# Third of five graph layers: edge projection and edge transposes ahead of the node products in TensorE's order

## The reference, cut to what matters

```
def _sage_conv(x, src, dst, Wl, b, Wr):
    agg  = segment_sum(x[src], dst)            # sum of the neighbours' rows
    cnt  = segment_sum(ones, dst)
    mean = agg / maximum(cnt, 1)[:, None]
    return mean @ Wl + b + x @ Wr

x = layernorm(x + conv2(relu(conv1(x))))                 # layers a1, a2: 128 -> 128 -> 128
x = layernorm(x + conv3(relu(conv2(relu(conv1(x))))))    # layers b1, b2, b3: 128 -> 256 -> 256 -> 128
```

## Time and profile before

| what | us |
|---|---|
| median of 3 runs | 5009.95 (5004.19 to 5011.4) |
| the profiled execution's own time | 5021.73 |
| its span (first to last instruction) | 5020.1 |
| TensorE busy in the span | 4645.7 (93%) |
| VectorE busy | 3822.4 (76%) |
| ScalarE busy | 2614.3 (52%) |
| stage of the third layer, 1634 to 2540 us after the start | 906 |
| stage of the fourth layer, 2541 to 3977 | 1436 |

### The profile page before, as it was taken

How to read it: one execution, slowest core, us unless ns; L and a number is a source line. 1 busy time by engine, 2 the same in 40 slices (tenths; PEclk the granted TensorE clock), 3 DMA queues, 4 the chain that set the end, 5 groups by cost and what they waited for, 6 DMA issues and landing times. The chain is left out here.

```text
span 5020.1 us, 145464 instructions
## 1 busy us (share of the span) xinstructions
PE 4645.7 (93%) x38674; PEld 4547.9 (91%) x38675; DVE 3822.4 (76%) x10162; ACT 2614.3 (52%) x7279; POOL 2329.1 (46%) x2182
## 2 busy tenths in 40 slices
PE   1788787999999899999989999999999899999998
PEld 1777776999999799999979999999999899999998
DVE  4566664777778699999967777777777588888888
ACT  1344443888988344444423333333333277777777
POOL 2666664555553444444344444444444343334331
PEclk9999898999999899999989999999999899999999
DMA  1667665888888566666668888888888788889887
GB/s 42 162 182 189 177 183 151 234 234 235 233 234 229 160 205 205 208 206 205 203 187 256 256 254 255 256 253 255 255 254 255 211 243 258 257 259 261 261 260 219
DMA packets 1454117, 1109.89 MB, mean 221 GB/s; under 512 B 76260, under 2 KB 1384833, under 8 KB 1454022
## 3 DMA queue, kind: packets, MB, share of 16 engines
q1 hardware_dynamic: 1377418, 927.61, 61.5%
q0 software_dynamic: 75712, 180.66, 14.5%
q10 hardware_dynamic: 892, 0.40, 0.0%
HBM read 696.86 MB, written 411.51 MB: 221 GB/s over the span
## 5 line engine op out<-in xcount | busy, mean ns | idle before, releaser
L1402 ACT ACTIVATE f_t_hi_b<-f_turned_b 128x512 fp32r<-128x512 f32 x588 | 332.3, 597 | 933.3 <-PE f_turned_b L1300 739.5
L1329 PE MATMUL f_product_b<-b_r_all,f_t_hi_b 128*128 128x256 f32 x2352 | 709.4, 302 | 1.1 <-DVE f_onehot_b L1450 1.1
L1442 DVE SCALAR_TENSOR_TENSOR f_t_lo_b<-f_turned_b,f_t_hi_b 128x512 fp32r<-128x512 f32 x588 | 388.1, 687 | 395.6 <-ACT f_t_hi_b L1402 326.5
L975 DVE TENSOR_TENSOR m_onehot_a<-iota_all,t_win_all 128x512 f32<-128x512 f32 (+1 forms) x588 | 455.9, 776 | 275.1 <-PE m_product_a L842 194.8
L753 POOL DMA_INDIRECT m_e_rows_b<-g,m_e_idx_b x392 | 395.7, 1009 | 574.9 <-ACT m_e_idx_b L881 506.0
L1331 PE MATMUL f_product_b<-b_r_all,f_t_hi_b 128*128 128x256 f32 x2352 | 660.5, 281 | 0.0
L1333 PE MATMUL f_product_b<-b_r_all,f_t_lo_b 128*128 128x256 f32 x2352 | 660.3, 281 | 0.0
L1255 POOL DMA_INDIRECT f_e_rows_b<-x,f_e_idx_b x392 | 392.8, 1002 | 508.0 <-ACT f_e_idx_b L1387 435.4
L1336 PE MATMUL f_product_b<-f_ring_b,f_onehot_b 128*128 x3136 | 621.8, 279 | 0.0
L1407 ACT ACTIVATE f_ring_b<-f_e_product_b,t_rec_all 128x256 f32 (+1 forms) x784 | 329.7, 472 | 526.2 <-PE f_e_product_b L1357 405.6
L753 POOL DMA_INDIRECT m_e_rows_a<-h,m_e_idx_a x392 | 398.2, 1016 | 390.0 <-ACT m_e_idx_a L881 311.4
(11 more groups left out here) (210 smaller groups left out, 12336.9 us busy)
## 6 DMA issues: line engine op xcount, KB each, us to landing
g<-f_rows_out_b SPq DMA_DIRECT2D x392, 512.0 KB
f_rows_in_b<-g SPq DMA_DIRECT2D x196, 512.0 KB
m_rows_in_b<-g SPq DMA_DIRECT2D x196, 512.0 KB
m_t_full_a<-in_x_flat_dram SPq DMA_DIRECT2D x196, 256.0 KB
h<-m_rows_out_a SPq DMA_DIRECT2D x196, 256.0 KB
m_rows_in_a<-h SPq DMA_DIRECT2D x196, 256.0 KB
m_res_in_a<-in_x_dram SPq DMA_DIRECT2D x196, 256.0 KB
x<-m_rows_out_a SPq DMA_DIRECT2D x196, 256.0 KB
```

What stands on the lines that cost most here:

```text
L975: v.tensor_tensor(onehot[:, s, n0:n0 + n, :], pr.iota[:, :].unsqueeze(1).to_broadcast([P, n, P]), pr.t_win2[:, bass.ds(g.n(0, WINDOWS) + n ...
L1329: pe.matmul(to, t_hi[:, s, k, cols], cv["r2"][:, k, 0, :], start=(t % per == 0 and k == 0), stop=False, skip_group_check=True)
L1402: act.activation(t_hi[:, s, k, :], turned[(s * kt + k) % 2][:, :], FUNC).then_inc(s_hi.sem, 1)
L1442: v.scalar_tensor_tensor(out=t_lo[:, s, k, :], in0=turned[(s * kt + k) % 2][:, :], scalar=0.0, in1=t_hi[:, s, k, :].bitcast(F32), op0=ZERO_OP,
```

## The change

The third layer gets the flag that the fourth already has. On TensorE alone, `places(g)` and `multiply(g, 0)` move behind `project` and `turn_edges`; the step becomes `turn_nodes(g+1)`, `project(p-1)`, `turn_edges(p+1)`, `places(g)`, `multiply(g, 0)`, `multiply(g, 1)`. No instruction is added or removed, and no other engine's order changes.

```
-            dict(name="b1", h=x1, out=g1, relu=False, w=1, f_out=256, turned=False, Wl=b_wl1, Wr=b_wr1, b=b_b1),
+            dict(name="b1", h=x1, out=g1, relu=False, edges_first=True, w=1, f_out=256, turned=False, Wl=b_wl1, Wr=b_wr1, b=b_b1),
```

## The result

The changed kernel takes 5129.4 us (median of 4 runs, 5121.3 to 5135.68) against 5007.07 (4999.8 to 5011.4) of the kernel before in the same comparison: ratio 1.0249 [1.0237, 1.0262], 122 us slower. The forecast was 20 us slower.

What follows compares the result with a forecast made beforehand. The prediction took the pace at which TensorE takes matmuls as the bound. A two-group loop of 5.00, 0.05 and 4.07 us gave 4.56 against 4.456 a group, +19.6 us over 188 groups: 5010 + 20 = 5030 us, range 5006 to 5050.

Steps and rivals of the forecast that it cites:

- `places` moves behind the edge transposes: TensorE's 592 ns register load: twelve matmuls, some 1.4 us, cover it; costed at nothing, uncovered at most 18 us in all.
- the projection moves from T + 1.62 to T + 0.35: T starts a group's node transposes; the projection waits for VectorE's ring low part, making 4.56 us a group, +19.6 us.
- the 20 to 30 named as the sign: Third layer's steady groups: TensorE waits for the ring's low part some 0.1 us a group, 20 to 30 us in all.
- the first rival: No stall: VectorE moves forward with its inputs and only the turn-end gaps go; 5004 us, chance 0.12.
- second rival: Faster outright: TensorE's matmul spacing falls to 0.113 us, gaining 28 us; 4982 us without the stall, chance 0.05.
- The one-hot matrices and the gather: TensorE's waits: one-hot matrices' gets 0.9 us looser, the gather's 1.2 us tighter, costed at nothing as gathers run ahead.
- The turn ends' gaps: Idle ahead of the node transposes at turn ends goes when the register load moves: 5.8 us, not added to the sum.
- The stalled projection at full clock: A weight load nothing hides after the projection's wait: 0 to 0.17 us a stall, up to 16 us; 0 taken.
- The third rival: Heavier stall: TensorE's signal reaches ScalarE 0.93 us late on every second group's node transposes; +44 us, 5074 us, chance 0.09.
- The fourth rival: The stall comes, but pieces closing up elsewhere in TensorE's group make up half; +7 to +14, 5017 to 5024 us, chance 0.08.

Runs made afterwards that it cites:

- nodes_proj: Kernel before with the projection, then the ring places' load, moved behind the node transposes, edge transposes staying between the product halves; 4888.56 against 4772.92 us, ratio 1.0242.
- quarter_store: Changed kernel storing one of four node tiles per group in the third layer, the rest filled behind its loop; 4.730 us a group, 5394.35 us with the fill.
- plain_new: Changed kernel with the third layer's GpSimd gathers replaced by SyncE's plain loads of fixed rows; 4869.68 against 4774.24 us, 4.935 us a group.
- low_early: Changed kernel with VectorE's low part of the ring moved two instructions earlier in the third layer; 4910.41 against 4774.24 us, ratio 1.0283, 5.139 us a group.
- load_behind_nodes: Kernel before with only the ring places' load moved behind the node transposes in the third layer; 5008.89 against 5008.36 us, ratio 0.9996, 4.428 us a group.
- early_load2: Changed kernel with VectorE's ring low part earlier and the ring places' load between node transposes and projection; 4776.67 against 4772.92 us, ratio 1.0006.

## Why the forecast was wrong

**The step that failed is "*`places` moves behind the edge transposes* ... twelve matmuls stand between ... and they cover it", costed at nothing.** The twelve matmuls are between in the program, but most of them are through, or held with it, when the load is made. The sequencer passes instructions on in order, and at a weight load whose semaphore hasn't come it stops; the register load behind it starts only with the release, 0.16 us behind the awaited instruction's end in five kernels in which the edge transposes are ahead of it, and in nodes_proj 0.11 us behind the projection's start. In the changed kernel that is 0.44 us behind the projection's start (mean of 90 groups), when the projection and the edge transposes have 0.5 us left; a load of 0.59 us and the 0.15 us to the product don't fit under that. The cover of the register load is the queued work behind the last wait that ends late, not all the work ahead of it. The forecast priced the loss of cover at 0.59 us once a turn; it is lost in every second group, and at 1.17 us. Two things were missed with it:
- The wait that now stands ahead of the load, edge transposes for the low part of the gathered rows, wasn't looked at, since TensorE's own waits show it nowhere. VectorE writes that low part next behind the ring's: 2007.79 + 0.41 = 2008.20, 0.17 us ahead of the load.
- The load was taken at 592 ns from the earlier trace rows. Its place moved into the store. The trace of before had the other duration, one layer on, in the order that the third layer was to get:

```profile
L1306 PEldq TENSOR_LOAD <-t_slot_all x189: 587/765/1945, 2601.3 to 3956.0; - x189
```

It costs nothing there because the ring's low part is 1.6 us early and nothing ahead of the load waits: the load starts 1.06 us behind the end of the gathered rows' low part (median of 188), not 0.16.

**The sum, term by term,** in us a group. The first two terms are differences between kernels; the last two are estimates from durations in the changed kernel and in quarter_store:

| term | from | us a group | x 188 |
|---|---|---|---|
| the ring's wait | 4.589 - 4.457 | 0.132 | 25 |
| a load of 0.59 us in the open | 4.730 - 4.589 | 0.141 | 27 |
| the store stretches it | (1.172 - 0.593) / 2 | 0.290 | 54 |
| ScalarE late behind the node transposes | (0.910 - 0.655) / 2 | 0.128 | 24 |
| sum | | 0.691 | 130 |
| measured | 5.122 - 4.457 | 0.665 | 125 |

The halves are for the loop over two groups, which closes once. The 1.172 is the mean load in the groups that wait and the 0.910 ScalarE's mean start behind T in those that don't, both in the changed kernel; 0.593 and 0.655 are the same two in quarter_store. As a test, plain_new has no late ScalarE and loads of 1.046 us in the groups that wait: 4.730 + 0.453 / 2 = 4.957; it measures 4.935. The terms aren't wholly independent: without the ring's wait (low_early) the loads are longer still, 1.40 us, and the distance is the same.

**Right:** *the projection moves from T + 1.62 to T + 0.35* and waits for the ring's low part; it starts 0.05 us behind the low part (2007.87 to 2007.93), and the loop alone is 4.589 us against 4.56. That the view's 27.3 us fell into the 20 to 30 named as the sign is luck: the projection is 52 us late in all, partly because ScalarE is late and VectorE's chain with it. The order of VectorE's step sets the loop, as the first rival denied; the first and second rival didn't come. *The one-hot matrices and the gather* cost nothing: no row of the waits names them. The turn ends' gaps do go when the load moves (5.5 us in load_behind_nodes, 5.8 forecast), but only where nothing holds it.

**The stalled projection at full clock,** bounded at 0 to 0.17 us: from its first matmul to the edge transposes it takes 0.816 us in groups that wait and 0.795 in those that don't, so 0.02 us; the value taken, nothing, was near. The 107 ns that the Trainium skill ("TensorE: Matmul & The Clock Gate", section "LDWEIGHTS (loading the stationary operand)") gives for a weight load isn't seen whole: the measured 0.02 decides.

**The third rival,** TensorE's signal late on the node transposes, with 0.09, was partly right: the late signals moved from the projection to the node transposes of the groups that don't wait. By the estimate above it costs 24 us, half of the 44 worked out for it: 54 of the 92 groups that don't wait are hit. Most groups hit have a gather's instruction over the transposes' end (2012.63 to 2013.63 above, ScalarE at 2013.96), and without gathers it's gone. A gather there isn't enough: 116 groups of the changed kernel have one and are on time, and in low_early and nodes_proj, which gather too, no group is hit. How GpSimd and TensorE's signal come together stays open.

**The fourth rival** didn't come. The range ended at 5050 because no case in it had the load in the open in each loop; the note "without that cover it would cost at most its own 0.59 us once a turn" had closed that door.

## What to carry to other kernels

Before a register load of the sequencer is moved, mark each semaphore wait on its engine that it is moved behind, and ask how early each signal comes: with all of them early it was free at both places tried (load_behind_nodes, early_load2), behind one that comes just in time it is in the open, and its cover is only what is queued behind that wait. A wait can be late for the sequencer and invisible in the engine's waits, while the matmuls ahead of it run. Take the duration of such a load from the phase to which it moves, and look at all its durations in the trace, not at the place where it stands now.

## What the hardware showed that I hadn't expected

- A register load from SBUF (TENSOR_LOAD on TensorE's sequencer) takes 0.59 us with the DMA engines full of gathers and loads (339 GB/s), and 1.0 to 1.4 us, up to 1.92 (low_early), while a 512 KB store from SBUF to HBM is in flight. With a quarter of the store it is 0.59 us again. The Trainium skill ("DMA: Bandwidth & Descriptors", section "Latency and other measured facts") gives `tensor_load` a floor of some 600 ns; the shortest here, 587 ns, agrees. In the changed kernel no load with 10 or more of the store's packets in flight stayed under 0.8 us.
- TensorE's sequencer runs ahead of the matmuls past ready work, 1.0 us in the median of load_behind_nodes, and not at all past a weight load that waits: in nodes_proj the load starts 0.11 us behind the released projection. The Trainium skill ("TensorE: Matmul & The Clock Gate", section "Architectural detail: the array is 16× 32×32, not 1× 128×128") gives TensorE a queue of 64 and lets it pull weight loads ahead of matmuls that run; here neither helped what stood behind a waiting one.
- ScalarE's start behind TensorE's last transpose, 0.04 us as a rule, is up to 0.7 us late in 54 of 92 groups of the changed kernel, mostly with a gather instruction of GpSimd over that end (2013.41 to 2013.96 above), and not without gathers (0.66 us behind T in plain_new, against 0.91).
